# ScalarE issues the stores of the stage of rows; SyncE keeps the loads

## What is computed

```python
W = weights[condition]                            # (B, 128, 128)
x = x + jnp.einsum('bct,bcd->bdt', x, W)          # layer 0
u_m = x * mask[:, None, :]
kernel = _get_kernel(log_dt, C, log_A_real, A_imag, Lq)
y = irfft(rfft(u_m, 2 * L) * rfft(kernel, 2 * L))[..., :Lq]
x = x + (y + u_m * D[:, None]) * mask[:, None, :] # layer 1
```

## Time and profile before

| | us |
|---|---|
| median of 3 runs | 2551.11 |
| lowest, highest | 2542.53, 2554.0 |
| span of the profiled execution | 2540.9 |
| stage of rows, from the first load to the last eviction of row 131 | 8.6 to 474.8 |

### The profile page before, as it was taken

One profiled execution on the slowest core, in us unless ns is written; L12 is line 12 of the kernel. 1 busy time (PEld: TensorE's weight loads), 2 busy tenths in 40 slices (PEclk: granted clock), 3 DMA queues, 4 the chain that ended last, 5 costly groups with the idle time before them and its releaser, 6 DMA issues.

```text
span 2540.9 us, 61617 instructions
## 1 busy us (share of the span) xinstructions
PE 2225.9 (88%) x15101; PEld 1926.6 (76%) x15101; DVE 2042.8 (80%) x4125; ACT 1682.3 (66%) x4864; POOL 1249.5 (49%) x1492
## 2 busy tenths in 40 slices
PE   4667656788888899898889898899999999999999
PEld 1222222578787888787878887889999999999999
DVE  3899101488888889898898998888888888888887
ACT  3434544577777777777777777766666666666666
POOL 0893310265656566666565666553333333333332
PEclk9998999899999999999999999999999999999999
DMA  7888898878878788787787887876777777777776
GB/s 260 310 299 296 303 308 303 277 268 262 270 263 271 264 277 273 269 268 267 262 274 261 273 272 269 262 242 210 217 216 217 215 217 215 217 216 217 217 216 190
DMA packets 278052, 648.07 MB, mean 255 GB/s; under 512 B 31362, under 2 KB 146308, under 8 KB 278020
## 3 DMA queue, kind: packets, MB, share of 16 engines
q1 hardware_dynamic: 278020, 647.71, 78.6%
HBM read 328.82 MB, written 318.77 MB: 255 GB/s over the span
## 4 chain that ended last, share of the span: by engine, by line
PE 51%; DMA 21%; issue 12%; DVE 8%; ACT 3%; SPq 3%; ACTq 2%; DVEq 1%; POOL 0%
DMA toep<-k_scratch 11%; PE bank L890 10%; PE bank L892 9%; PE bank L891 9%; DMA row_x<-in_x 9%; PE bank L932 6%; PE bank L872 6%; DVE decay L796 5%; PE bank L924 5%; PE bank L859 4%; DVE e_lo L775 2%; ACTq L522 1%; ACT t_hi L618 1%; ACT row_y L547 1%; SPq L341 1%
## 5 line engine op out<-in xcount | busy, mean ns | idle before, releaser
L890 PE MATMUL bank<-t_hi,u_hi 128*128 128x256 f32 x1024 | 362.2, 354 | 121.7 <-DVE decay L796 121.7
L859 PE MATMUL bank<-row_x,w_sel 128*128 128x512 f32 x528 | 290.5, 680 | 178.5 <-DMA row_x<-in_x 118.2
L784 DVE TENSOR_TENSOR u_lo<-bank,u_hi 128x512 fp32r<-128x512 f32 x512 | 351.0, 686 | 107.2 <-ACT u_hi L597 107.1
L547 ACT ACTIVATE row_y<-bank 128x512 f32<-128x512 f32 x512 | 303.2, 592 | 184.2 <-PE bank L859 184.0
L779 DVE TENSOR_TENSOR t_lo<-toep,t_hi 128x256 fp32r<-128x256 f32 x256 | 314.9, 1230 | 127.1 <-ACT t_hi L618 127.0
L465 POOL COPY par<-table 128x72 f32 (+1 forms) x256 | 120.1, 469 | 569.7 <-PE bank L892 487.1
L932 PE MATMUL bank<-toep,u_odd 128*128 128x128 f32 x2048 | 394.9, 274 | 0.0
L606 ACT ACTIVATE state<-bank 128x128 f32<-128x128 f32 x768 | 214.3, 279 | 270.2 <-PE bank L924 180.1
L859 PEld LDWEIGHTS bank<-row_x,w_sel 128*128 128x128 f32 x528 | 99.4, 209 | 366.7 <-issue 183.9
L796 DVE COPY_PREDICATED decay<-mask,bank 128x512 f32<-128x512 uint8 x512 | 373.7, 730 | 0.8 <-PE bank L892 0.6
L468 POOL TENSOR_TENSOR outer<-par 128x256 f32<-128x256 f32 x512 | 316.4, 639 | 20.5
(11 more groups left out here) (145 smaller groups left out, 6244.8 us busy)
## 6 DMA issues: line engine op xcount, KB each, us to landing
row_x<-in_x SPq DMA_DIRECT2D x256, 512.0 KB, 6.1
x_scratch<-row_y SPq DMA_DIRECT2D x256, 512.0 KB, 4.1
decay<-x_scratch SPq DMA_DIRECT2D x256, 512.0 KB, 5.6
out<-decay SPq DMA_DIRECT2D x256, 512.0 KB, 3.4
toep<-k_scratch SPq DMA_DIRECT2D x256, 128.0 KB, 4.7
k_scratch<-k_pad SPq DMA_DIRECT2D x128, 192.0 KB, 5.8
b_scratch<-b_whole SPq DMA_DIRECT2D x128, 128.0 KB, 3.7
b_whole<-b_scratch SPq DMA_DIRECT2D x128, 128.0 KB, 4.9
```

The source lines that it names most:

```text
L547: nc.scalar.activation(row_y[j][:, q * BANK:(q + 1) * BANK], from_bank[:, :], ACT.Copy).then_inc(row_taken, 1)
L784: v.tensor_tensor(u_lo[j % 2][:, blocks, :], t_bank[q][:, :].rearrange("s (k b) -> s k b", b=B), u_hi[j % 2][:, blocks, :].bitcast(fp32), ...
L859: mm(to_bank[:, :], w_sel[j][:, :], row_x[j][:, q * BANK:(q + 1) * BANK], start=True, stop=True).then_inc(row_made, 1)
L890: mm(to, w_hi, m_hi, start=start, stop=False, skip_group_check=True)
```

## The change

In the stage of rows, ScalarE issues the store of row n itself, behind the eviction of the row's second half, after waiting on its own `row_taken`. The store goes to ScalarE's DMA queue. SyncE's list there holds loads alone, each with its wait on `row_made`. The last group of rows (128 to 131) is written out on every engine, since its store has another target. The stage of channels is as before: SyncE issues its stores of rows.

```diff
-            for first, last, share in zip((1,) + SETUP, SETUP + (ROWS_FIRST // SLOTS,), setup + (None,)):
+            for first, last, share in zip((1,) + SETUP, SETUP + (GROUPS,), setup + (None,)):
...
+            for g in range(GROUPS, ROWS_FIRST // SLOTS):
+                group(g)
@@ SyncE, rows
                     load_row(n, j, seg, n if seg == 0 else n - B)
-                    if not (isinstance(n, int) and n < 2):
-                        of = seg if not (isinstance(n, int) and n - 2 < B) else 0
-                        store_row(n - 2, (j + 2) % SLOTS, of, n - 2 if of == 0 else n - 2 - B)
@@ SyncE, end of the stage
             for k in range(2):
                 load_x1(0, k, k, 0)
-            for n in (ROWS_FIRST - 2, ROWS_FIRST - 1):
-                store_row(n, n % SLOTS, 1, n - B)
@@ ScalarE, rows
                     for q in range(NQ):
-                        take_row(g * SLOTS + j, j, q, bank[(j % 2) * NQ + q])
+                        take_row(n, j, q, bank[(j % 2) * NQ + q])
...
+                    act.wait_ge(row_taken, n * NQ + NQ)
+                    act.dma_start(x1_dram[seg][bass.ds(b, 1), 0:H * SEG].rearrange("a (h t) -> (a h) t", t=SEG), row_y[j][:, :]).then_inc(x1_stored[j], 16)
```

More of the change, by code:

```diff
@@ L550, in rows @@
                 for j in range(SLOTS):
+                    n = g * SLOTS + j
                     for q in range(NQ):
-                        take_row(g * SLOTS + j, j, q, bank[(j % 2) * NQ + q])
+                        take_row(n, j, q, bank[(j % 2) * NQ + q])
                         if q == 0:
-                            pick_w(g * SLOTS + (j + 1), (j + 1) % SLOTS)
+                            pick_w(n + 1, (j + 1) % SLOTS)
+                    seg, b = (0, n) if not (isinstance(g, int) and g >= GROUPS) else (1, n - B)
+                    act.wait_ge(row_taken, n * NQ + NQ)
+                    act.dma_start(x1_dram[seg][bass.ds(b, 1), 0:H * SEG].rearrange("a (h t) -> (a h) t", t=SEG), row_y[j][:, :]).then_inc(x1_stored[j], 16)
             def keep_parameters():
```

## The result

| | us |
|---|---|
| before, median of 4 runs | 2548.84 |
| changed, median of 4 runs (2459.47 to 2479.62) | 2471.91 |
| ratio, 95% interval | 0.969 (0.967 to 0.972) |
| span of the profiled execution, before and after | 2540.9, 2464.6 |

The change makes the kernel 3.1% faster, about twice the forecast gain and outside the range. The spans differ by 76.3 us. The stage of rows is 80.7 us shorter: the last eviction of row 131 ended at 474.8 us before and ends at 394.1 now. The rest of the program took 4.4 us more in these two executions (2070.5 after 2066.1).

A forecast was written before the change was run, and what follows sets the result against it. The prediction took a latency loop with three loads in flight to bound the stage of rows. It summed 34 us from faster rows and 4 us at the stage's end: 2551.1 - 38 = 2513 us, range 2490 to 2538.

The forecast's parts named there:

- What bounds the kernel now: Stage of rows: a latency loop with three loads in flight sets the pace, 3.45 us a row, not DMA capacity.
- The loop with four loads stops being the bound: Stage of rows: with four loads in flight the load loop takes 2.2 us a row, far below 3.45.
- The DMA engines: Stage of rows: next bound, 3.05 us a row at a share of 0.96, so 3.18; saves 34 us.
- The last sentence of the prediction: A price per packet that changes when loads and stores come from two queues would make the sum wrong; no size.
- The loop between ScalarE and TensorE: Stage of rows: 2.63 us a row when data is there, below 3.05, so it sets the pace only in patches.
- What it costs ScalarE: Waits and store issues in the stage of rows: costed at nothing, an issue of 0.35 us hidden with 0.29 spare.
- Rival 2: Stage of rows: the store issue holds up ScalarE, 3.77 us a row, 41 us lost, 2588 us; chance 0.09.
- The end of the stage: Row 132's load follows the channel loads, over 5 us sooner, so ScalarE's 4.08 us idle goes; 4 us saved.
- Rival 3: Stage of rows: loads and stores from two queues fill each other's gaps; 87 us saved, 2464 us; chance 0.07.
- rival 1: Stage of rows: DMA engines already the bound at 0.89, so no change; 2535 to 2551, time 2544 us; chance 0.14.

The follow-up runs named there:

- e8: The kernel before with every store one row late in SyncE's list instead of two, so two loads in flight: 2733.24 us, in a single run.
- e1: The kernel before with every store four rows late in SyncE's list instead of two, one queue, four loads in flight: 2438.88 us, ratio 0.9575.
- e12: The kernel before, with the weights picked two rows ahead instead of one: 2556.3 us, ratio 1.0015.
- e3: The changed kernel, with the weights picked two rows ahead instead of one: 2434.67 us, ratio 0.9562.
- e5: e1 with the weights picked two rows ahead instead of one: 2421.21 us, ratio 0.9497.
- e9: e11 with ScalarE also issuing a small DMA per row behind its wait, row stores still in SyncE's queue: 2476.74 us, ratio 0.9729.
- e11: e1 with ScalarE waiting after each row for its own second eviction but issuing nothing, a repeat run: 2448.6 us, ratio 0.9599.
- e4: The changed kernel as it is, measured again on another chip: 2468.34 us, ratio 0.9714 to the kernel before.
- e6: The changed kernel, with ScalarE's wait and store of a row moved behind the next row's first-half eviction and weight picking: 2496.61 us, ratio 0.9806.

## Why the prediction was wrong

**What bounds the kernel now: right.** The loop of three loads was the bound. e8 lengthens it with two loads and loses 185 us, part of it by a lower clock; e1 frees it by SyncE's order alone and gains 108; e12 leaves it and picks the weights earlier, for nothing.

**The loop with four loads stops being the bound: right.** PE's waits for loads are gone and SyncE waits for PE. The loads landed in 6.3 us and not in 9 (four loads of 3.2 us less 2.5 would be 10.3, not 9), because what came next was not their queue.

**The DMA engines: the step that failed.** The prediction says that one row costs the DMA engines 0.885 x 3.45 = 3.05 us and calls it the floor if a packet takes as long as now. It took the condition as given. The share was 0.96 forecast, 0.97 measured, but the same product is 2.79 us in the changed kernel and 2.65 to 2.68 in e1, e3 and e5. So 3.05 was no floor: share times pace measures how long transfers were in hand at that pace, not what the engines need for a row. A row was forecast at 3.18 us and took 2.88, which is 127 x 0.30 = 38 us, nearly all of the miss of 41. What set the 2.88 was the turn between ScalarE and TensorE: with the weights picked earlier, at the same share and more, a row takes 2.65 (e3). The row that told of it was there: single slices at 410 to 426 GB/s against stretches of 4 us at 301 to 327. I used the first only against the lower bound; e5 held that rate over 300 us. The last sentence of the prediction did name a changed price as what would make the sum wrong, but put it on the second queue, which e1 rules out.

**The loop between ScalarE and TensorE: sized rightly, ranked wrongly.** At 2.63 us it was held to be under the DMA engines' 3.05 and to matter in patches. With the DMA engines able to carry a row in 2.6 us (e5) it is the bound of most of the stage, and its mean length is 2.88: the rows at the turn of the loop take 3.30 us in the mean (four of them with other work of ScalarE between), the others 2.74.

**What it costs ScalarE: wrong.** It was costed at nothing, with 0.29 us to spare. The issue took 0.34 us as forecast, and the tight pattern does hide it. But wait and issue together cost 28 us between the medians of e9 and e11 (10 us in their traces), by the branch of the loop at least. The reckoning looked at a row inside the loop's body and not at the row where the body ends. Rival 2 named the mechanism of a store that holds up ScalarE. The prediction let that decide the pace only from an issue of 1.2 us on, against a pace of 3.18; at the real pace, which this loop itself sets, that point is gone.

**The end of the stage: not kept.** The load of row 132 came sooner, and ScalarE's 4.08 us of waiting for it fell to 0.65. But PE stands 3.64 us for the channel loads, which wait for the landing of row 127's store, now 6.2 us after its issue instead of 3.6. The stage of rows lost 80.7 us and the kernel 76.3. Whether the rest of the program became longer at all is open: in e4, the same kernel, it took 2060.6 us, 5.5 less than before. The 4 us are within what one execution differs from another.

**The rivals.** Rival 3 gave 2464 and the time came to it, in part by luck: its mechanism, two queues that fill each other's gaps, is not the one, since one queue does better (e1). It was loads that no longer stand behind an eviction. Its bound, a loop of ScalarE and TensorE at 2.8 us a row, is what the trace shows at 2.88. The Trainium skill's rule in "DMA: Bandwidth & Descriptors", section "Issuing engines are not separate DMA queues", says that transfers issued by several engines run on the same 16 DMA engines, and that issuing from more than one saves only the sequencer's time to issue. The runs agree that a second queue brings no rate: 398 GB/s in one queue (e1), 365 and 398 in two (changed, e3). By that rule alone the change would have brought next to nothing, the time of rival 1; whether the engines were full, it doesn't say. What it counts as saved, the sequencer's time to issue, was not what this change saved; it was a wait in that sequencer's list. Rival 1 falls with the 365 GB/s.

## What to carry to other kernels

When loads and stores are issued by one engine in order, look at which wait stands ahead of each load, and compare it with what frees the load's buffer. Issue each store late enough in the list that its wait is over before the next load's buffer comes free (here four rows late instead of two), before moving stores to an engine that computes: that gave 4.2% where the move gave 3.1%. Don't take the busy share of the DMA engines times the pace for what a transfer costs them: it came out at 3.04 us in the kernel before and at 2.65 in the fastest ones. Look for the rate of the fastest slices instead. And don't take a share near 1 for a proof that they are the bound: see who waits for whom. And where an engine gets a further instruction, check its slack at the turn of its loop as well as inside it.

## What the runs showed of the hardware

- One core's loads and stores together ran at 413 GB/s over 300 us (e5), with stretches at 420, while DVE and POOL were busy; the stage ran at 303 before.
- The DMA engines' busy time for the same 1 MB (load and store) was 3.18, 3.04 and 2.68 us with two, three and four loads in flight in one queue (e8, before, e1).
- Their busy share was 0.97 at 340 GB/s (e6), 0.97 at 365 (changed) and 1.02 at 413 (e5).
- Reading one value into a register on ScalarE's queue took 0.27 to 1.78 us, with medians from 0.28 (e8) to 0.90 (e6) for the same instruction.
- With ScalarE issuing 4 KB a row the kernel took 0.973 of the time before (e9), with 512 KB a row 0.971 (e4).
